# The first norms of layers 0 and 1, slot by slot and split between ScalarE and VectorE

## What is computed

```python
x = _layernorm(x + _L0_gnn_ref(x, adj, ...))   # A_hat x, linear, batch norm, relu, linear, batch norm
x = _layernorm(x + _L1_gnn_ref(x, ..., adj, src, dst))   # edge attention over 256 edges, 4 heads
x = _layernorm(x + _L2_gnn_ref(x, adj, adj, W1, W2, W3)) # three graph convolutions, hidden 256 and 512
x = _layernorm(x + _L3_gnn_ref(x, adj, W, a))            # dense graph attention

def _layernorm(x, axis=-1, eps=1e-05):
    m = jnp.mean(x, axis=axis, keepdims=True)
    v = jnp.var(x, axis=axis, keepdims=True)
    return (x - m) / jnp.sqrt(v + eps)
```

## Time and profile before

| | |
|---|---|
| median of 3 runs | 638.22 (638.16 to 639.72) |
| the profiled execution, device time | 637.05 |
| its span, first to last instruction | 635.1 |
| mean granted TensorE clock | 0.93 |
| busy PE / PEld | 553.0 (87%) / 488.5 (77%) |
| busy DVE / ACT / POOL | 422.8 (67%) / 367.1 (58%) / 217.7 (34%) |
| instructions PE / DVE / ACT / POOL | 3508 / 1446 / 733 / 253 |

### The profile page before, as it was taken

The page is one execution under the profiler, slowest core; times in us unless marked ns, Lnnn a source line. Parts: engine busy times, 40 slices in busy tenths (PEclk is TensorE's granted clock), DMA queues, the critical chain, the costliest instruction groups (busy, mean ns, idle before and its releaser), DMA issues.

```text
span 635.1 us, 11295 instructions
## 1 busy us (share of the span) xinstructions
PE 553.0 (87%) x3508; PEld 488.5 (77%) x3508; DVE 422.8 (67%) x1446; ACT 367.1 (58%) x733; POOL 217.7 (34%) x253
## 2 busy tenths in 40 slices
PE   2999797789998799998998999899799799799372
PEld 2888443568886798988988889889789789789262
DVE  5588586788882644685585575675675675755895
ACT  1566692576653245366666666666665765663660
POOL 6840520565663312314215215215215115103231
PEclk9999799699998799999899899799899899799777
DMA  5223000321100000000001001000000000100002
GB/s 178 87 79 99 2 0 0 98 57 45 33 1 0 2 1 1 1 1 1 1 2 35 0 1 33 0 0 23 10 0 12 22 0 1 33 1 9 26 2 66
DMA packets 28382, 15.25 MB, mean 24 GB/s; under 512 B 2320, under 2 KB 28048, under 8 KB 28352
## 3 DMA queue, kind: packets, MB, share of 16 engines
q1 hardware_dynamic: 27792, 13.65, 7.5%
q0 software_dynamic: 560, 1.25, 0.5%
HBM read 10.69 MB, written 4.19 MB: 23 GB/s over the span
## 4 chain that ended last, share of the span: by engine, by line
PE 71%; DVE 12%; ACT 9%; issue 4%; POOL 2%; DMA 1%; SPq 1%; DVEq 0%; ACTq 0%; POOLq 0%
PE psum L237 13%; PE psum L238 12%; PE psum L239 12%; PE psum L1496 8%; PE psum L1321 5%; PE psum L1363 4%; ACT soft L1178 4%; ACT ob L231 3%; PE psum L1448 2%; PE psum L1370 2%; PE psum L1374 2%; PE psum L1384 2%; PE psum L1438 2%; DVE ln_st L183 2%; PE psum L1542 2%
## 5 line engine op out<-in xcount | busy, mean ns | idle before, releaser
L202 POOL TENSOR_TENSOR ln_r<-ln_v,mhalf 128x8 f32<-128x8 f32 x32 | 53.8, 1681 | 257.6 <-DVE ln_v L196 257.6
L1496 PE MATMUL psum<-l2w_s,h 128*128 128x128 f32 x512 | 59.7, 275 | 0.0
L1496 PEld LDWEIGHTS psum<-l2w_s,h 128*128 128x128 f32 x512 | 59.0, 192 | 0.7
L1165 ACT ACTIVATE h<-psum 128x512 f32<-128x512 f32 x64 | 37.3, 596 | 33.4 <-PE psum L239 33.4
L237 PE MATMUL psum<-qt_hi,l2w_s_hi 128*128 128x512 f32 x128 | 52.6, 411 | 0.0
L238 PE MATMUL psum<-qt_lo,l2w_s_hi 128*128 128x512 f32 x128 | 50.5, 394 | 0.0
L239 PE MATMUL psum<-qt_hi,l2w_s_lo 128*128 128x512 f32 x128 | 50.5, 394 | 0.0
L231 ACT ACTIVATE keep_x<-keep_x,ln_b,ln_r (+1 forms) x112 | 45.9, 483 | 1.4 <-POOL ln_b L205 1.4
L854 DVE TENSOR_TENSOR s_lo<-psum,s_hi 128x512 fp32r<-128x512 f32 x16 | 11.1, 692 | 47.5 <-ACT s_hi L1169 47.5
L183 DVE BATCH_NORM_STATS2 ln_st<-keep_x 128x6 f32<-128x128 f32 (+1 forms) x192 | 39.1, 277 | 2.9 <-ACT keep_x L1092 1.6
L237 PE MATMUL psum<-l2w_s_hi,pt_hi 128*128 128x256 f32 x64 | 22.4, 350 | 19.6 <-DVE pt_lo L839 19.6
(11 more groups left out here) (225 smaller groups left out, 1824.9 us busy)
## 6 DMA issues: line engine op xcount, KB each, us to landing
xin<-in_x SPq DMA_DIRECT2D x64, 128.0 KB, 2.2
out_x<-ob SPq DMA_DIRECT2D x32, 128.0 KB, 1.8
l2w_raw<-in_l2w POOLq DMA_DIRECT2D x1, 512.0 KB, 6.7
adjs<-in_adj SPq DMA_DIRECT2D x1, 256.0 KB, 2.7
adjs<-in_adj_t SPq DMA_DIRECT2D x1, 256.0 KB, 2.9
l2w_s<-in_l2w POOLq DMA_DIRECT2D x1, 256.0 KB, 6.5
w_raw<-in_w_t SPq DMA_DIRECT2D x1, 128.0 KB, 3.2
w2t<-in_w_t SPq DMA_DIRECT2D x1, 128.0 KB, 3.2
```

The source lines that it names most:

```text
L202: pool.tensor_tensor(ln.r[:].rearrange("p s k -> p (s k)"), ln.v[:].rearrange("p s k -> p (s k)"), mhalf[:], ALU.pow).then_inc(ln.root, 1)
L1165: act.activation(h2[:, s, g, :], bank(4 + g)[:, 0, :], ACT.Relu).then_inc(h2_out, 1)
L1496: i = pe.matmul(bank(s)[:, 0, k * D:(k + 1) * D], h2[:, s, g, j * N + t * P:j * N + (t + 1) * P], l2w3_s[:, g, :], start=(g == 0), stop=(g ...
```

## The change

For the first step of layers 0 and 1 the norm is done slot by slot. Statistics, aggregation and epsilon of one slot are `first_stats`, its power `first_power` (128x4 values, one GpSimd instruction, no negated mean and no product), its normalising `first_apply`, always on VectorE. The split is no longer GpSimd's: ScalarE copies the high part (`first_high`), VectorE subtracts for the low one (`first_low`). The semaphores of `LayerNorm` get a set of their own for these two steps, so the counts of the later steps are one lower (`late`).

In layer 0 VectorE's order becomes: sum slot 0, its statistics, sum slot 1, its statistics, normalise slot 0, sum slot 2, low part of slot 0, normalise slot 1, low part of slot 1, sum slot 3, and then norm 1. TensorE's order stays there. At the end of layer 1 TensorE turns the attention between the two slots of projection IT-2, does output1(0,0) before attend1(0,1), splits the last projection around output1(0,1), puts the last `score` behind attend1(1,0), and moves attend1(1,1) into `step(0)`, behind `hidden1` of slot 0. The core of the diff:

```diff
+        def first_stats(dve, s, ln):
+            dve.wait_ge(ln.added, s + 1)
+            for k in range(4):
+                i = dve.bn_stats(ln.st[:, s, k, :], xn[:, s, k // 2, k % 2, :])
+            i.then_inc(ln.one_stats, 1)
+            dve.wait_ge(ln.one_stats, s + 1)
+            for k in range(4):
+                i = dve.bn_aggr(ln.ag[:, s, k, :], ln.st[:, s, k, :])
+            i.then_inc(ln.one_mean, 1)
+            dve.wait_ge(ln.one_mean, s + 1)
+            dve.tensor_scalar(ln.v[:, s], ln.ag[:, s, :, 1], LN_EPS, None, ALU.add).then_inc(ln.one_var, 1)
+        def first_power(pool, s, ln):
+            pool.wait_ge(ln.one_var, s + 1)
+            pool.tensor_tensor(ln.r[:, s], ln.v[:, s], mhalf[:, 0:4], ALU.pow).then_inc(ln.one_rstd, 1)
+        def first_apply(dve, s, ln, done, by):
+            dve.wait_ge(ln.one_rstd, s + 1)
+            for k in range(4):
+                y = xn[:, s, k // 2, k % 2, :]
+                i = dve.tensor_scalar(y, y, ln.ag[:, s, k, 0:1], ln.r[:, s, k:k + 1], ALU.subtract, ALU.mult)
+            i.then_inc(done, by)
+        def first_high(act, s, done, value, to, ok):
+            act.wait_ge(done, value)
+            act.activation(to[:, s], xn[:, s], ACT.Copy).then_inc(ok, 1)
+        def first_low(dve, s, high, ok, to, low):
+            dve.wait_ge(ok, s + 1)
+            dve.tensor_tensor(to[:, s], xn[:, s], high[:, s], ALU.subtract).then_inc(low, 1)
...
-            ln_power(pool, 0, ln0)
-            for s in range(2):
-                split_x1(0, s, True)
+            for s in range(2):
+                first_power(pool, s, ln0)
             ln_power(pool, 1, ln0)
...
-            ln_power(pool, 0, ln1)
-            for s in range(2):
-                split_x(0, s, True)
+            for s in range(2):
+                first_power(pool, s, ln1)
...
-            sum0(0)
-            variance0(0, True)
-            sum0(1)
-            apply0(0)
+            for s in range(2):
+                sum0_slot(0, s)
+                first_stats(dve, s, ln0)
+            for s in range(2):
+                first_apply(dve, s, ln0, ln0_done[s], 2)
+                if s == 0:
+                    sum0_slot(1, 0)
+                first_low(dve, s, x1s[0], x1_hi, x1s[1], x1_lo)
+            sum0_slot(1, 1)
             variance0(1, False)
...
+            both_low(0)
+            add(0, 0, o1_done, 1, ln1)
+            first_stats(dve, 0, ln1)
+            add(0, 1, o1_done, 6, ln1)
+            first_stats(dve, 1, ln1)
+            first_apply(dve, 0, ln1, ln1.done, 1)
+            leaky(IT - 1)
+            first_low(dve, 0, xs[0], xs_hi, xs[1], xs_lo)
+            first_apply(dve, 1, ln1, ln1.done, 1)
+            both_low(1)
+            first_low(dve, 1, xs[0], xs_hi, xs[1], xs_lo)
+            take_scores(1)
...
-            add(0, 0, o1_done, 1, ln1)
-            add(0, 1, o1_done, 6, ln1)
-            variance(0, ln1, True)
-            take_scores(1)
-            both_low(1)
-            apply(0, ln1)
...
-            scale0(0)
+            for s in range(2):
+                first_high(act, s, ln0_done[s], 2, x1s[0], x1_hi)
             bn_out(3, False)
...
-            for s in range(2):
-                projected(IT - 1, s)
-            for s in range(2):
-                weighted_high(1, s, False)
+            projected(IT - 1, 0)
+            weighted_high(1, 0, False)
+            projected(IT - 1, 1)
+            weighted_high(1, 1, False)
+            for s in range(2):
+                first_high(act, s, ln1.done, s + 1, xs[0], xs_hi)
...
-            project(IT - 2)
+            project_slot(IT - 2, 0)
             turn_attention(0)
+            project_slot(IT - 2, 1)
             gather(IT - 1, False)
...
-                    if ahead and not first:
+                    if first and s == 1:
+                        pe.wait_ge(sm, SM_STEPS + 1)
+                    if ahead and not (first and s == 0):
                         attend1(p + 1, s, 6 + s)
...
             pe.wait_ge(ln0.added, Q)
+            output1(0, 0, 1)
             attend1(0, 1, 0)
-            project(IT - 1)
-            output1(0, 0, 1)
+            project_slot(IT - 1, 0)
             output1(0, 1, 6)
-            score(IT - 1)
+            project_slot(IT - 1, 1)
             pe.wait_ge(ln1.added, 2)
             attend1(1, 0, 6)
-            pe.wait_ge(sm, SM_STEPS + 1)
-            attend1(1, 1, 7)
+            score(IT - 1)
```

More of the change, by code:

```diff
@@ L160, in build, with __init__ @@
         class LayerNorm:
-            def __init__(self, tag):
+            def __init__(self, tag, late):
+                self.late = late
                 names = ("added", "stats", "mean", "var", "rstd", "done")
@@ L172, in __init__ @@
                 self.root = sem(f"ln{tag}_root")
-        ln0, ln1, ln2, ln3 = (LayerNorm(k) for k in range(4))
+                self.one_stats, self.one_mean, self.one_var, self.one_root, self.one_rstd = (
+                    (sem(f"ln{tag}_one_{k}") for k in ("stats", "mean", "var", "root", "rstd")) if late else [None] * 5)
+        ln0, ln1, ln2, ln3 = (LayerNorm(k, 1 if k < 2 else 0) for k in range(4))
         ln0_done = [sem("ln0_done0"), sem("ln0_done1")]
@@ L184, in ln_stats @@
             i.then_inc(ln.stats, 2)
-            wait_apart(dve, dc, ln.stats, 2 * p + 2)
+            wait_apart(dve, dc, ln.stats, 2 * p if ln.late else 2 * p + 2)
             for s in range(2):
@@ L191, in ln_var_eps @@
         def ln_var_eps(dve, p, ln):
-            dve.wait_ge(ln.mean, p + 1)
+            dve.wait_ge(ln.mean, p if ln.late else p + 1)
             dve.tensor_scalar(ln.m[:].rearrange("p s k -> p (s k)"), ln.ag[:].rearrange("p s k c -> p (s k) c")[:, :, 0],
@@ L199, in ln_power @@
         def ln_power(pool, p, ln):
-            pool.wait_ge(ln.var, p + 1)
+            pool.wait_ge(ln.var, p if ln.late else p + 1)
             pool.tensor_tensor(ln.r[:].rearrange("p s k -> p (s k)"), ln.v[:].rearrange("p s k -> p (s k)"), mhalf[:],
                                ALU.pow).then_inc(ln.root, 1)
-            pool.wait_ge(ln.root, p + 1)
+            pool.wait_ge(ln.root, p if ln.late else p + 1)
             pool.tensor_tensor(ln.b[:].rearrange("p s k -> p (s k)"), ln.m[:].rearrange("p s k -> p (s k)"),
                                ln.r[:].rearrange("p s k -> p (s k)"), ALU.mult).then_inc(ln.rstd, 1)
+        def first_stats(dve, s, ln):
[24 more added lines that the diff above has]
+            dve.tensor_tensor(to[:, s], xn[:, s], high[:, s], ALU.subtract).then_inc(low, 1)
         def ln_root(act, p, ln):
@@ L219, in ln_apply @@
         def ln_apply(dve, y, dst_of, p, s, ln):
-            dve.wait_ge(ln.rstd, p + 1)
+            dve.wait_ge(ln.rstd, p if ln.late else p + 1)
             for k in range(4):
@@ L227, in ln_scale @@
         def ln_scale(act, y, p, s, ln):
-            act.wait_ge(ln.rstd, p + 1)
+            act.wait_ge(ln.rstd, p if ln.late else p + 1)
             for k in range(4):
@@ L486, in split_x1 @@
                     pool.wait_ge(g_done, q - 1)
+                    pool.wait_ge(x1_lo, q)
                 pool.tensor_copy(x1s[0][:, s], xn[:, q]).then_inc(x1_hi, 1)
@@ L521, in split_x @@
                     pool.wait_ge(pt_done, q - 1)
+                    pool.wait_ge(xs_lo, q)
                 pool.tensor_copy(xs[0][:, s], xn[:, q]).then_inc(xs_hi, 1)
@@ L715, in apply, with sum0_slot @@
                     ln_apply(dve, row(p), lambda t, j: row(p)(s, t, j), p, s, ln)
+            def sum0_slot(p, s):
+                q = 2 * p + s
+                dve.wait_ge(t1_done, q + 1)
+                dve.wait_ge(x_in2[s], 32 * (p + 1))
+                dve.tensor_tensor(xn[:, q], bank(s)[:, 0, :].rearrange("p (t j d) -> p t j d", t=T, j=2),
+                                  xin[:, s], ALU.add).then_inc(ln0.added, 1)
             def sum0(p):
                 for s in range(2):
[L720 to L725, removed]
+                    sum0_slot(p, s)
             def leaky(p):
@@ L741, in apply0 @@
             def apply0(p):
-                dve.wait_ge(ln0.rstd, p + 1)
+                dve.wait_ge(ln0.rstd, p)
                 for k in range(4):
@@ L816, in _, with add @@
             leaky(IT - 2)
+            def add(p, s, done, psum_bank, ln):
+                q = 2 * p + s
+                dve.wait_ge(done, q + 1)
+                dve.tensor_tensor(xn[:, q], bank(psum_bank)[:, 0, :].rearrange("p (t j d) -> p t j d", t=T, j=2), xn[:, q],
+                                  ALU.add).then_inc(ln.added, 1)
             def weighted_low(p, s):
@@ L827, in _ @@
             both_low(0)
-            leaky(IT - 1)
[L830 to L835, removed]
+            add(0, 0, o1_done, 1, ln1)
[3 more added lines that the diff above has]
+            first_apply(dve, 0, ln1, ln1.done, 1)
+            leaky(IT - 1)
+            first_low(dve, 0, xs[0], xs_hi, xs[1], xs_lo)
[3 more added lines that the diff above has]
+            take_scores(1)
```

(12 more changed lines are left out.)

## The result

The changed kernel takes 644.35 (median of 5 runs, 641.34 to 644.88) where the kernel before takes 638.22. The ratio is 1.008 (95% interval 1.0054 to 1.0106): slower. Measured again later it is 1.0077 (1.0053 to 1.0101). That execution is the shortest of the five and the one with the highest mean grant of TensorE's clock (0.929; the other four 0.922 to 0.923 and 642.73 to 644.88).

The account below looks back on a forecast made before the run. The prediction took a chain 71% TensorE, with the start of step 1's statistics setting the pace in layer 0. Its terms, 1.7 + 1.3 = 3.0, gave 640.05 on the profiled execution, forecast 641.2 from the median; range 638.4 to 644.2.

Parts of the forecast that it names:

- First place, +1.7: Layer 0's norm start: statistics of step 1 start 2.4 later, 0.7 comes back, so the second gather is 1.7 later.
- the 0.7 given back: Layer 0: the mean's negation, 0.86 beside GpSimd's split, no longer stalls once that split is gone, saving 0.7.
- the load of the input: Layer 0: SP's load of step 2's slot 1 lands near 124.5, before VectorE wants it at 125, costing nothing.
- Second place, +1.3: Layer 1 to layer 2: attend1(1,0) waits for the weighted low part, scores behind it; net 1.2 to 1.4 later.
- The lock: Rival, 0.22: in both places tensor_scalar waits for GpSimd's power, adding 0.65 and 1.3, so 643.2.
- by 134.1: Layer 0: TensorE's first gather, a turn and a projection end by then, before the second gather at 136.0.
- the sum of 3.0: Both places together: 1.7 at the first plus 1.3 at the second, added to the execution time.
- its two known stretches: Second place: TensorE's lower clock costs 2.4 before 210 and about 3.8 in the second stretch.
- faster: Rival, 0.12: the lower clock vanishes from the second place, 3.0 - 6.2 = -3.2, so 635.0.
- a later rise: TensorE's clock rises later than assumed; the forecast's own range, 639.8 to 642.6, allows a sooner or later rise.
- first place only: Rival, 0.13: the second place comes out even because TensorE's clock rises sooner after 217, so 639.9.
- clock even: Rival, 0.11: both lower-clock stretches of the second place shorten, so 638.6, no change that can be told.

Follow-up runs that it names:

- sums_early: Changed kernel with VectorE's sum of slot 3 and statistics of step 1 moved ahead of both low parts in the first place; 1.0017 to the kernel before.
- wlow_early: Changed kernel with the weighted low part of slot (1,0) moved ahead of the first normalising on VectorE in the second place; 1.0016 to the kernel before.
- score_ahead: Changed kernel with the last scores put back ahead of attend1(1,0) in TensorE's program; 1.0016 to the kernel before.
- fill_short: Changed kernel plus six idle product calls on TensorE between the first projection and the second gather; 1.008 to the kernel before.
- after_again: The changed kernel, unaltered, measured and profiled once more beside the short filler; 1.0077 to the kernel before.
- first_only: Changed kernel with the second place undone, so the first place of the change alone; 1.0041 to the kernel before.
- second_only: Changed kernel with the first place undone, so the second place of the change alone; 1.0030 to the kernel before.
- first_reordered: Changed kernel with statistics of step 1 ahead of the low parts and the second place as in the kernel before; 0.9971 to the kernel before.
- both_moves: Changed kernel with statistics of step 1 ahead of the low parts and the weighted low part ahead of the normalisings; 633.95, 0.9948 to the kernel before.

## Why the prediction came out as it did

The forecast was 641.2 (638.4 to 644.2, slower with 0.66). The sign is right, the median lies 0.15 above the range. That the profiled execution, 641.34, lies next to 641.2 is luck: in it a term that the sum did not have (below) and the 1.4 that came back cancel. Term by term:

**First place, +1.7: 1.67.** The statistics of step 1 are 2.39 late (2.4), the negation of the mean takes 0.17 and stalls no more (the 0.7 given back), the first gather stands at 122.78 behind a turn (122.6), the second gather is 1.67 late. sums_early shows that the cause is the named one. log_a held the first high copy until 117.54, or 117.2 without the 0.32, as in the working; the load of the input changed nothing: VectorE's sum at 124.61 did not wait.

**Second place, +1.3: 1.64.** xs_lo is ready at 218.5 and attend1(1,0) starts at 220.28; less the 3.53 by which the place starts late, 215.0 and 216.8 (215.3 and 217.2). Layer 2 starts at 221.9 by the same count (222.0). The 0.3 missing is in the products behind it: 8.5 from there to the output product, where the working had 7.9. wlow_early and score_ahead confirm the mechanism. Turning the attention earlier brought nothing, as worked out.

**The lock: did not happen.** The four tensor_scalar at 115.62 took 1.11 for all with a GpSimd power beside them (115.79, 1.04), and so at 215.59 (power at 215.76). By the Trainium skill (SBUF — State Buffer, Who interferes with whom) those behind the first, which had started ahead of the power, would be held until its end; here they were not. The value 0 taken for the unknown cost was right, and the 0.22 given to this rival bought only the upper end of the range.

**What failed: the step that let TensorE end "by 134.1" ahead of the second gather, and with it the hole of 1.9 that this implied.** I took an upper bound of TensorE's work there, which was harmless for the start of the gather, and never asked how long a hole the real end leaves. TensorE was done at 133.1, the hole was 3.14, and the gather behind it ran at the lower clock: 1.54 that the sum of 3.0 did not have, and the profiled execution shows 4.3. The trace of before could have warned, if not decided: a hole of 2.89 had the lower clock behind it at 216.24 and the upper one at 134.26, and the working took up only the first. I had allowed the clock to shift only inside the second place, in its two known stretches, and mostly towards less: both rivals with another clock (even, faster) pointed down, so that the range had nothing above but the lock and a later rise.

**What it is worth at the end is less clear.** fill_short took the 1.5 away where it arose and the time stayed. The medians differ by 6.1, the two holes explain 3.3. The rest goes along with TensorE's clock: over the whole executions measured beside fill_short the changed kernel was granted 0.922 to 0.928 and before 0.927 to 0.932, and in after_again, granted 0.922, some 2 of the 6.6 arose behind 310, far from both places. Each of first_only and second_only is above its term too. That an execution can have its lower stretches elsewhere is shown; that they make up the rest is argued from these grants, and why the changed kernel has more of them in sum stays open.

The rivals "first place only" (second_only is slower by itself), "clock even" and "faster" fell (0.50 over 220.2 to 226, right behind the hole).

## What to carry to other kernels

A step done in halves gives a gain only to the instruction that really stands next in the queues: before splitting, ask whose date sets the round (here the next step's statistics, and the attention ahead of layer 2), and put the new operations behind it, not in front. The order inside one engine decided the sign: the same operations gave 1.008 and 0.9948. And when a change makes or lengthens a wait of TensorE, price the clock behind the hole, upwards as well, but don't take a local gain of clock for one at the end.

## What the runs showed of the hardware

GpSimd's power of 128x4 values took 1.01 to 1.05, of 128x8 1.64 to 1.68: half the data cost 0.6 less, not half. Beside it VectorE's tensor_scalar and its two-operand subtraction both ran at full pace, though beside GpSimd's split tensor_scalar waited (3.39 for eight where four alone took 1.12).

The lower clock came in the second gather in each profile with a hole of 3.07 to 3.14 ahead of it (after, after_again, first_only, second_only, wlow_early, score_ahead), and not in those with 2.89 (before) or with 1.02 to 1.26 (first_reordered, both_moves, sums_early), nor where products filled the hole. Its 16 products took 5.4 to 5.5 or 3.7 to 4.0. The length of a hole does not decide alone: the 2.89 at 216.24 in before was followed by the lower clock.
